# A fused cross-attention and mixture-of-experts block: the other bank and order for the up blocks, x2's low part, the variance and the third pair moved, and the negated row maxima made on GpSimd

## The reference, cut to what matters

```python
# x: 32 items of 256 rows x 256; ctx: 32 x 77 x 256; mask: 32 x 77 (False = the key is cut)
x = x + attn(ctx, layernorm(x), mask)          # 4 heads of 64; keys are 256 rows of x and 77 of ctx
x = x + ffn(layernorm(x))

# attn: xn = layernorm(ctx)*g+b, ln = layernorm(latents)*g+b; q = ln@W_q; k, v = [xn; ln]@W_kv
sim  = (rmsnorm(q)*64**-0.5) @ rmsnorm(k).T    # keys that are cut get -max
out  = softmax(sim) @ v @ W_out + b_out

# ffn: a shared part of width 512 and 8 experts of width 128; the router picks 2 of 8 for each row
r      = relu(x @ up.T)**2
routed = einsum('tei,ehi,te->th', r, down_weights, cw)
shared = relu(x @ shared_up.T)**2 @ shared_down.T
```

## Time and profile before

| | us |
|---|---|
| median of 3 runs (lowest, highest) | 1199.18 (1198.08, 1201.65) |
| the profiled execution, own time | 1199.88 |
| its span, first to last instruction | 1198.1 |
| PE busy | 1158.1 (97%) |
| DVE busy | 1021.4 (85%) |
| ACT busy | 790.8 (66%) |
| POOL busy | 547.9 (46%) |

### The profile page before, as it was taken

One profiled execution on the slowest core, in us unless ns is written; L12 is line 12 of the kernel. 1 busy time (PEld: TensorE's weight loads), 2 busy tenths in 40 slices (PEclk: granted clock), 3 DMA queues, 4 the chain that ended last, 5 costly groups with the idle time before them and its releaser, 6 DMA issues.

```text
span 1198.1 us, 32986 instructions
## 1 busy us (share of the span) xinstructions
PE 1158.1 (97%) x11772; PEld 1073.1 (90%) x11772; DVE 1021.4 (85%) x3500; ACT 790.8 (66%) x1900; POOL 547.9 (46%) x473
## 2 busy tenths in 40 slices
PE   7799999999999999999999999999999999999997
PEld 6699999999989999999999999999999999999997
DVE  6689888888988888888889888899888898888876
ACT  5567766667766667666767666667666677666673
POOL 5444445445445345444345444444454444454442
PEclk9899999999999999999999999999999999999999
DMA  5000000000000000000000000000000000000000
GB/s 181 2 13 22 23 22 22 2 22 22 22 22 22 2 23 22 23 22 23 2 22 23 22 22 12 12 22 23 22 23 10 13 23 22 23 22 5 8 10 18
DMA packets 28145, 26.06 MB, mean 22 GB/s; under 512 B 6544, under 2 KB 27440, under 8 KB 27984
## 3 DMA queue, kind: packets, MB, share of 16 engines
q1 hardware_dynamic: 27904, 23.83, 6.4%
q0 software_dynamic: 80, 0.14, 0.1%
HBM read 15.57 MB, written 8.39 MB: 20 GB/s over the span
## 4 chain that ended last, share of the span: by engine, by line
PE 56%; DVE 18%; ACT 13%; issue 11%; ACTq 1%; DMA 0%; DVEq 0%; POOL 0%; SPq 0%
PE attn_ps L411 7%; ACT probs L676 6%; PE up_ps L295 5%; PE up_ps L297 5%; PE up_ps L296 5%; PE attn_ps L397 5%; PE down_ps L295 5%; PE down_ps L297 4%; PE down_ps L296 4%; PE attn_ps L295 4%; PE attn_ps L297 4%; PE attn_ps L296 4%; DVE acc L1065 3%; ACT relu_sb L721 3%; DVE k_lo L892 2%
## 5 line engine op out<-in xcount | busy, mean ns | idle before, releaser
L1262 POOL TENSOR_TENSOR hid_lo<-relu,hid_hi 128x512 fp32r<-128x512 f32 x192 | 247.2, 1288 | 268.3 <-DVE hid_hi L1050 158.0
L1065 DVE SCALAR_TENSOR_TENSOR acc<-down_ps,route_w,acc 128x256 f32<-128x256 f32 x512 | 222.0, 475 | 15.9 <-PE down_ps L297 15.3
L295 PE MATMUL down_ps<-down_hi,hid_hi 128*128 128x256 f32 x768 | 234.0, 305 | 1.4 <-ACT hid_hi L726 0.8
L295 PE MATMUL up_ps<-x_hi,up_hi 128*128 128x256 f32 x768 | 225.9, 294 | 7.9 <-DVE x_lo L974 7.7
L297 PE MATMUL down_ps<-down_hi,hid_lo 128*128 128x256 f32 x768 | 216.6, 282 | 0.0
L296 PE MATMUL down_ps<-down_lo,hid_hi 128*128 128x256 f32 x768 | 216.3, 282 | 0.0
L296 PE MATMUL up_ps<-x_lo,up_hi 128*128 128x256 f32 x768 | 214.4, 279 | 0.0
L297 PE MATMUL up_ps<-x_hi,up_lo 128*128 128x256 f32 x768 | 214.4, 279 | 0.0
L676 ACT ACTIVATE probs<-masked,neg_max,q_scale 128x333 f32<-128x333 f32 x256 | 168.5, 659 | 68.3 <-DVE neg_max L911 68.3
L295 PEld LDWEIGHTS up_ps<-x_hi,up_hi 128*128 128x128 f32 x768 | 144.5, 188 | 16.1 <-issue 9.8
L295 PEld LDWEIGHTS down_ps<-down_hi,hid_hi 128*128 128x128 f32 x768 | 145.1, 189 | 13.9 <-issue 12.8
(11 more groups left out here) (145 smaller groups left out, 2856.9 us busy)
## 6 DMA issues: line engine op xcount, KB each, us to landing
out<-acc SPq DMA_DIRECT2D x31, 256.0 KB, 2.2
x_first<-in_x SPq DMA_DIRECT2D x16, 256.0 KB, 2.7
w_stage<-in_x SPq DMA_DIRECT2D x16, 256.0 KB, 2.8
up_stage<-in_up_t SPq DMA_DIRECT2D x1, 1536.0 KB, 7.5
down_stage<-in_down_t SPq DMA_DIRECT2D x1, 1536.0 KB, 8.6
c_first<-in_ctx SPq DMA_DIRECT2D x16, 77.0 KB
w_stage<-in_ctx SPq DMA_DIRECT2D x16, 77.0 KB
w_stage<-in_w_kv SPq DMA_DIRECT2D x1, 512.0 KB, 5.4
```

The lines of the kernel that those rows point to most:

```text
L295: nc.tensor.matmul(out_ap, s_hi, m_hi, start=first, stop=False)
L1065: nc.vector.scalar_tensor_tensor(acc[:, t, :], down_ps[:, (e + 1) % 2, t * D:(t + 1) * D], route_w[:, t, e:e + 1], acc[:, t, :], ALU.mult, ...
L1262: nc.gpsimd.tensor_tensor(hid_lo[:, p % HID_RING, :], relu2[:, p % 2, :], hid_hi[:, p % HID_RING, :], ALU.subtract).then_inc(hid_lo_done, 1)
```

## The change

Six edits, made in every step:

1. The banks of `up_ps` are swapped for the pairs, the transposed layer norm and the spread inverse sums. An even p now uses bank 1. Therefore the wait for `q_low` (which reads bank 0) moves from `up(b, 0)` to `up(b, 1)`.
2. On DVE `x2_low(b)` stands before `q_low(b+1)`.
3. On DVE the two variance instructions are cut out of `layer_norm1` into `variance1`, which stands behind the first four `mask_scores`.
4. On ACT `hidden(b-1, 2)` (the third pair) stands before the first softmax block, not behind the second.
5. `negate_max` is made on POOL, by a product with `neg_scale`, a negated copy of `q_scale` that POOL makes once in a step. `mask_keys` on DVE gets a wait for the masks of its item.
6. On POOL the order is now: q_scale, neg_scale, low(0), low(1), negate_max 0, low(2), rstd_first, negate_max 1, residual, low(3), low(4), and so on. `residual` stood second before.

```diff
@@ tensor
-                        nc.tensor.transpose(up_ps[:, ft, t * P:(t + 1) * P], x_hat[:, t, ft * P:(ft + 1) * P], ident[:])
+                        nc.tensor.transpose(up_ps[:, 1 - ft, t * P:(t + 1) * P], x_hat[:, t, ft * P:(ft + 1) * P], ident[:])
...
                 if p == 0:
                     pe.wait_ge(x2_hi_done, (b + 1) * FT)
                     pe.wait_ge(x2_lo_done, (b + 1) * FT)
-                    if following:
-                        pe.wait_ge(q_lo_done, b + 2)
+                if p == 1 and following:
+                    pe.wait_ge(q_lo_done, b + 2)
...
-                        last = split_product(up_ps[:, p % 2, j * S:(j + 1) * S], (up_hi[:, k, cols], up_lo[:, k, cols]),
+                        last = split_product(up_ps[:, (p + 1) % 2, j * S:(j + 1) * S], (up_hi[:, k, cols], up_lo[:, k, cols]),
@@ scalar, step
                 ffn(1)
+                ffn(2)
                 softmax(b, 0, first)
                 softmax(b, 1, first)
-                ffn(2)
@@ vector
+            def variance1(b, first):
+                dve.wait_ge(ln1_step, b * LN1_STEPS + LN1_STEPS)
                 if not first:
                     dve.wait_ge(rstd1_done, b)
                 nc.vector.tensor_scalar(var1[:, 0:T], mv1[:, 0:T, 1], 1.0 + LN_EPS, LN_EPS * LN_EPS, ALU.mult, ALU.add)
...
             def mask_keys(b):
                 dve.wait_ge(mask_loaded, b * DMA + DMA)
+                if b > 0:
+                    dve.wait_ge(masked_done, b * U)
@@ vector, step
                 mask_scores(b, 3, first)
-                negate_max(b, 0)
+                if following and not first:
+                    variance1(b + 1, False)
...
                 mask_scores(b, 7, first)
-                negate_max(b, 1)
...
+                x2_low(b)
                 q_low(b + 1)
-                x2_low(b)
@@ gpsimd
                 inverse_root(q_scale[:], q_norm[:], q_scale_done)
+                pool.wait_ge(q_scale_done, b + 1)
+                nc.gpsimd.tensor_scalar(neg_scale[:], q_scale[:], -1.0, None, ALU.mult).then_inc(neg_scale_done, 1)
+
+            def negate_max(b, t):
+                cols = slice(t * H, (t + 1) * H)
+                pool.wait_ge(masked_done, b * U + (t + 1) * H)
+                pool.wait_ge(neg_scale_done, b + 1)
+                nc.gpsimd.tensor_tensor(neg_max[:, cols], row_max[:, cols], neg_scale[:, cols],
+                                        ALU.mult).then_inc(neg_max_done, 1)
@@ gpsimd, step
                 q_scales(b, first)
-                residual(b, first)
...
                 low(0)
+                low(1)
+                negate_max(b, 0)
+                low(2)
                 if following and not first:
                     rstd_first(b + 1, False)
-                for p in range(1, 5):
-                    low(p)
+                negate_max(b, 1)
+                residual(b, first)
+                low(3)
+                low(4)
```

More of the change, by code:

```diff
@@ L102, in build @@
         q_scale = sb("q_scale", [P, U])
+        neg_scale = sb("neg_scale", [P, U])
         k_sq = sb("k_sq", [KC, CH, D])
@@ L210, in build @@
         rstd1_done, ln_lo_done, x_res_done = sem("rstd1_done"), sem("ln_lo_done"), sem("x_res_done")
+        neg_scale_done = sem("neg_scale_done")
         q_scale_done, k_scale_done, rstd2_done, hid_lo_done = sem("q_scale_done"), sem("k_scale_done"), sem("rstd2_done"), sem("hid_lo_done")
@@ L312, in transpose_ln @@
                     for t in range(T):
-                        nc.tensor.transpose(up_ps[:, ft, t * P:(t + 1) * P], x_hat[:, t, ft * P:(ft + 1) * P], ident[:])
-                    nc.tensor.transpose(up_ps[:, ft, S:KEYS], c_hat[:, ft * P:(ft + 1) * P],
+                        nc.tensor.transpose(up_ps[:, 1 - ft, t * P:(t + 1) * P], x_hat[:, t, ft * P:(ft + 1) * P], ident[:])
+                    nc.tensor.transpose(up_ps[:, 1 - ft, S:KEYS], c_hat[:, ft * P:(ft + 1) * P],
                                         ident[0:C, 0:C]).then_inc(lnt_ps, 1)
@@ L426, in spread_inverse @@
                         u = t * H + 2 * ft
-                        last = nc.tensor.transpose(up_ps[:, 0, ft * S + t * P:ft * S + (t + 1) * P],
+                        last = nc.tensor.transpose(up_ps[:, 1, ft * S + t * P:ft * S + (t + 1) * P],
                                                    inv_wide[:, u:u + 2, :], ident[:])
@@ L634, in ln_full @@
                     for k, cols in enumerate((slice(0, S), slice(S, KEYS))):
-                        last = nc.scalar.activation(ln_t[:, ft, cols], up_ps[:, ft, cols], ACT.Identity,
+                        last = nc.scalar.activation(ln_t[:, ft, cols], up_ps[:, 1 - ft, cols], ACT.Identity,
                                                     bias=ln_b[:, k, ft:ft + 1], scale=ln_g[:, k, ft:ft + 1])
@@ L689, in inverse_out @@
                     act.wait_ge(attn_done, b)
-                nc.scalar.activation(inv_t[:], up_ps[:, 0, :].rearrange("p (f s) -> p f s", f=FT),
+                nc.scalar.activation(inv_t[:], up_ps[:, 1, :].rearrange("p (f s) -> p f s", f=FT),
                                      ACT.Copy).then_inc(inv_done, 1)
@@ L720, in hidden @@
                 act.wait_ge(up_done, b * PAIRS + p + 1)
-                nc.scalar.activation(relu_sb[:, p % 2, :], up_ps[:, p % 2, :], ACT.Relu).then_inc(relu_done, 1)
+                nc.scalar.activation(relu_sb[:, p % 2, :], up_ps[:, (p + 1) % 2, :], ACT.Relu).then_inc(relu_done, 1)
                 act.wait_ge(relu_done, b * PAIRS + p + 1)
@@ L823, in layer_norm1 @@
                     nc.vector.bn_aggr(mv1[0:rows, t, :], stats1[0:rows, t, :]).then_inc(ln1_step, 1)
-                dve.wait_ge(ln1_step, k + LN1_STEPS)
+            def variance1(b, first):
+                dve.wait_ge(ln1_step, b * LN1_STEPS + LN1_STEPS)
                 if not first:
@@ L905, in mask_scores @@
                                                ALU.add, ALU.max, row_max[:, u:u + 1]).then_inc(masked_done, 1)
[L907 to L912, removed]
             def invert_sums(b, t):
@@ L1176, in _ @@
             layer_norm1(0, True)
+            variance1(0, True)
             normalize1(0, True)
@@ L1191, in _ @@
             layer_norm1(1, False)
+            variance1(1, False)
             k_normalize(0, 0, True)
```

## The result

The changed kernel took 1204.08 us (median of 13 runs, 1201.96 to 1207.86), the kernel before 1200.07 us (13 runs, 1198.08 to 1201.68). The ratio is 1.0035, with a 95% interval of 1.0023 to 1.0048: slower by 4.0 us, where 9.9 had been forecast (8.4 + 1.5). The side was right, the size was not. The profiled execution of the changed kernel, 1201.96 us with a span of 1200.2, is the fastest of its runs; against that of before (1199.88) it is 2.1 us longer.

The account below looks back on a forecast made before the run. PE, busy 97%, was taken as the bound, with DVE's chain having only 0.42 us to spare. The profiled 1199.88 + 8.4 + 1.5 = 1209.8, less 0.7 for the median, gave 1209.1 us; range 1183 to 1216.

Parts of the forecast that it names:

- PE's gain, 0.56 us a step: On PE, waits behind pt_out on ACT and x2_low on DVE go, together 16.7 us or 0.56 us a step.
- Masks first, variance held: On DVE, masks start at about 602.8, the variance is held until about 605.2, routing starts at 605.3, 0.8 us ahead.
- Two holds on the routing: On DVE, low(2) holds routing levels until 607.65, and x_res on POOL, 1.29 us, holds the stretch of mask_keys and levels 9 to 12.
- the third rival: POOL's power also holds DVE's routing, up to 0.8 us a step, 24 us on top, 1233 us; chance 0.03.
- DVE's lag, 0.7 us: On DVE at add_shared, the chain runs 0.7 us behind the kernel before, with 0.5 to 0.9 as ends.
- What is late next: The lag passes to add_expert(2); down_expert(4) on PE starts at 619.92 against 619.64, 0.28 us later, +8.4 us over 30 steps.
- DVE's slack of 0.42 us: DVE's add_expert(2) has only about 0.42 us to spare before PE's down_expert(4) needs it.
- The first rival, 1184: On DVE, low(2) or x_res costs nothing, the lag becomes -0.5 us and PE gets all 0.56 us: 1184 us; chance 0.36.
- The rival in between, 1199 to 1202: Holds overlap more, a DVE lag of 0.3 to 0.5 us gives back what PE wins, no change; chance 0.15.
- The first step, +1.5: In the first step, negate_max behind four down_lo on POOL makes the first pt_out later, +1 to +2 us once, 1.5 taken.

Follow-up runs that it names:

- the fastest version: Changed kernel with x_res second on POOL after the first step, first step's first negation behind the first down_lo, masks 4 to 7 ahead of routing levels 4 to 8: 1173.12 us.
- the first experiment: Changed kernel with x_res made second on POOL, right behind neg_scale, in all steps but the first: 1178.03 us, ratio 0.9828.
- half of the residual: Changed kernel with x_res made for the first 128 rows only, in its old place, in all steps but the first: 1186.84 us, ratio 0.990.
- second, third pair back: Changed kernel with x_res second on POOL in all steps but the first and ffn(2) behind softmax 1 on ACT again: 1184.43 us, ratio 0.9878.
- the experiment with the early first negation: Changed kernel with the first step's first negation on POOL behind the first down_lo instead of the fourth: 1199.72 us, ratio 1.0006.

## Why the forecast was right in direction and wrong in size

**PE's gain, 0.56 us a step: mechanism right, the size read too small.** Both waits went. But the view of waits counts only the time behind a matmul's modelled end. Here are, before, after, with the residual second, and in the fastest version, the last transposes ahead of `down_expert(4)` and its first product (timelines of PE; the product of before is in the earlier trace rows):

```profile
619.40 0.49 PE L397 MATMUL attn_ps<-ident,probs 128*111 128x128 f32 x3
```

```profile
622.01 0.49 PE L399 MATMUL attn_ps<-ident,probs 128*111 128x128 f32 x3
```

```profile
609.57 0.49 PE L399 MATMUL attn_ps<-ident,probs 128*111 128x128 f32 x3
610.00 0.36 PE L297 MATMUL down_ps<-down_hi,hid_hi 128*128 128x256 f32 x1
```

```profile
641.36 0.49 PE L399 MATMUL attn_ps<-ident,probs 128*111 128x128 f32 x3
641.60 0.36 PE L297 MATMUL down_ps<-down_hi,hid_hi 128*128 128x256 f32 x1
```

From start to start that is 0.24, 0.72, 0.43 and 0.24 us. Without a wait it is 0.24. The changed kernel thus waits 0.48 us where the view says 0.23, and the first experiment 0.19 us where it says nothing. Rows of 0.28 us that start 0.12 apart hide that much. At `down_expert(2)` it is 619.89 - 619.45 = 0.44 us, where the view says 0.17 and 0.12 would be no wait. The fastest version needs 35.29 us a step, the kernel before 36.19: PE had at least 0.90 us to give, not 0.56. Laid over the fastest version row by row, the step before has about 0.3 us more ahead of `up(b, 0)`, 0.5 at the transposes behind `pt_out`, and 0.15 at the transposed layer norm, which the view doesn't list. This did not spoil the forecast, which took the end from DVE. But it is why the residual's move took 0.77 us from a step instead of the expected 0.55: DVE's `add_expert(2)` came 0.74 us earlier, about as expected, and PE could follow it all the way.

**Masks first, variance held: right.** The masks start at 605.77 - 2.99 = 602.78 (forecast 602.8), the routing at 605.21 (605.3).

**Two holds on the routing: right, and this was the decisive doubt.** A plain two-input row of 4 or 16 columns is held by POOL's 512-column operations, 1.23 and 1.29 us. The Trainium skill (SBUF — State Buffer, section "SBUF: two separate sides") says so of a DVE instruction with two SBUF inputs, and the trace agrees. By its wording the power, which reads SBUF as well, should have held level 7; it did not (0.16 us beside 0.87), so the third rival, POOL's power, is refuted.

**DVE's lag, 0.7 us: the step that failed.** It was 0.47 to 0.52 us. The forecast had masks 4 to 7 start at 608.4, end at 610.25, and `add_shared` start at 612.9. They start at 608.14, end at 609.93, and `add_shared` starts at 612.57: a lag of 0.52 us against before, and of 621.72 - 2.99 - 618.26 = 0.47 at `add_expert(2)`. The error sits at the first hold. I counted 1.1 of the 1.87 us of levels as done ahead of `low(2)`, and all the rest as still to come behind it. But the routing came 0.1 us sooner, and the row that is held has done its own work when the hold ends: behind 610.75 only levels 7 and 8 were left, 0.38 us instead of 0.75. I had allowed for such an overlap once, with 0.15 us, where there are two holds. The stretch with the second hold came out near the reckoning, and 0.1 us too long: from 609.93 to 612.57 are 2.64 us, against 2.66 less 0.15. A gap of 0.11 us stands there ahead of `mask_row`, from 612.92 to 613.03. It is probably the wait that edit 5 gives to `mask_keys`, which the prediction had put at nothing; no run tested it alone.

**What is late next: right in kind, with luck in its sign.** By the view, PE waits behind `hid_lo` and `acc`, and nowhere else in a step. `down_expert(4)` starts at 622.73 - 2.99 = 619.74, 0.10 us later than before and not 0.28. The step became 0.06 us longer, not 0.28. With DVE's lag at the low end of the stated 0.5 to 0.9, the step's cost of +2.4 us was in the text; the value taken was the middle. By the ruler, 29 steps cost 1.9 us, where 8.4 had been forecast for 30. The lag passed DVE's slack of 0.42 us by no more than 0.05 to 0.10 us; by the same reckoning the steady steps would have gained with a lag a tenth of a microsecond shorter. That the whole came out slower rests as much on the first step's 1.8 us.

That DVE's chain sets the step is shown by the kernels in which its length was changed. From the keys' transposes on PE to the start of `add_expert(2)` in one steady step, and the length of a step by the ruler, in us:

```
                              add_expert(2)   step    difference
with the residual second          20.73       35.48     14.75
half of the residual              20.96       35.71     14.75
changed, masks over low(2)        21.01       35.77     14.76
changed, third pair back          21.25       36.05     14.80
changed                           21.47       36.25     14.78
residual twice                    22.51       37.26     14.75
before                            21.00       36.19     15.19
second, third pair back           20.52       35.65     15.13
the fastest version               20.27       35.29     15.02
```

In six kernels a step is this addition's start plus 14.8 us, and in all six `down_expert(4)` starts over 0.4 us behind the first of the transposes ahead of it. The kernel before stands apart by 0.4, the slack that the forecast had read from the earlier trace rows. So do the last two, in which the distance is 0.24 to 0.25 as well: there PE does not wait for this addition. In the fastest version the addition waits for PE:

```profile
640.23 0.88 DVE L1064 SCALAR_TENSOR_TENSOR acc<-down_ps,route_w,acc 128x256 f32<-128x256 f32 x2 [0.25 <-PE down_ps L299]
```

**The first rival, 1184, fell for the changed kernel; its price was about right.** Take one hold away and the time is 1178.03 (`x_res`) or 1188.57 (`low(2)`, with `x_res` still holding a row). The lag at `add_expert(2)` is then 20.73 - 21.00 = -0.27 or 0.01 us, not the -0.5 of the rival; the first of these times lies below 1184 because PE had more to give than 0.56 us.

**The rival in between, 1199 to 1202, came nearest.** Its condition, a lag of 0.3 to 0.5 us because holds overlap more than was reckoned, is what the rows show, but for 0.02 us. The profiled execution, 1201.96, lies in its range, and the median, 1204.08, lies 2.1 us above it. It had been given 0.15, the forecast 0.46.

**The first step, +1.5: right.** POOL's `down_lo` ended at 34.23 (forecast 34.5 to 35), `pt_out` started at 37.03 (37 to 38), and `attn` of the second step came 1.8 us later. It wasn't foreseen that the clock would stay at its lower level 6.8 us longer. The medians differ by 4.0 us and the profiles by 2.1, and the changed kernel's runs spread over 5.9 us. Its three longest, 1207.34 to 1207.86, have the lowest mean granted clock, 0.987, its three shortest, 1201.96 to 1202.30, have 0.991; how much of the spread the clock makes was not measured by itself and stays open. The changed kernel is 3.7 us behind at 1134 and 2.1 at the end. The profile of before has a stretch at lower clock near its end (0.83 in 1170 to 1180) that the profile after has not; it is worth 1.7 us at most by the estimate above and can account for this.

## What to carry to other kernels

Where two engines share a memory, look for short instructions that last as long as another engine's large one, and lay instructions that aren't held (here those with a PSUM operand) over it; shortening a chain by moving one neighbour's operation can be worth more than taking work off. A list of waits is a lower bound when the engine's rows overlap: measure from start to start against a step without the wait. And count a hold from where the held row would have ended, not from where the hold begins, at each hold.

## What the runs showed that was not expected

- What POOL does decides over what it holds: additions and subtractions of 256 and 512 columns (0.73 to 1.30 us) held DVE rows of 2 to 128 columns until their end, with one SBUF input (`var`, `mask_row`) or two (the routing); a power of 128x3 (0.87 us) held none. Not every row is held beside an addition: the masks, with one input from PSUM, kept 0.50 us in every run, and an aggregate of the layer norm took its usual 0.18 us in the midst of `x_res` in the first experiment.
- A small product on POOL took 0.20 to 0.27 us in the changed kernel, the scaling by a constant 0.24 us, where 0.11 to 1.30 had bounded it. In the first step the same scaling of eight columns took 1.11 us (from 23.89 to 25.00), beside a subtraction of 768 columns on DVE that ended at 24.89. A product of four columns took 0.92 us in the experiment with the early first negation, where the kernel has such a DVE subtraction beside it. So POOL is held too.
- One edit changed its sign with the place of another: the early third pair made the kernel 6.7 us slower with `x_res` late on POOL and 6.4 us faster with it early.
